# Moving a norm ahead of the last settling, the embeddings' product between the last mixes, and two transposes behind the q/k projections, in an audio tower on one Trainium2 core

## What is computed

```python
def reference(x, ...):
    # tokens: 4096 patches of 200 samples -> spectrum -> two-layer MLP -> 128 features
    fr = jnp.fft.rfft(xp, axis=-1)
    feats = jnp.concatenate([jnp.abs(fr), jnp.angle(fr)], axis=-1)
    h = gelu(feats @ w1 + b1) @ w2 + b2
    # attention: 8 heads of 64, sequences of 256 tokens, 16 of them, sparsemax for softmax
    q, k, v = jnp.split(layernorm(h) @ W_qkv, 3, axis=-1)
    sim = jnp.einsum('bhid,bhjd->bhij', q, k) * SCALE
    z_sorted = jnp.flip(jnp.sort(sim, axis=-1), axis=-1)
    cssv = jnp.cumsum(z_sorted, axis=-1)
    k = jnp.sum(1.0 + r * z_sorted > cssv, axis=-1, keepdims=True)
    tau = (jnp.take_along_axis(cssv, k - 1, axis=-1) - 1.0) / k
    h = h + einsum(jnp.maximum(sim - tau, 0.0), v) @ W_out + b_out
    # experts: 8, each takes its 1024 best tokens of 4096 and adds to them
    return h + experts(layernorm(h))
```

## Time and profile before

| what | us |
|---|---|
| median of 3 runs (918.42 to 922.3) | 920.19 |
| the profiled execution, its time | 916.4 |
| its span, from the first instruction to the last | 914.3 |
| PE busy (share of the span) | 677.6 (74%) |
| DVE busy | 621.5 (68%) |
| ACT busy | 457.8 (50%) |
| POOL busy | 203.4 (22%) |
| POOL's waits for DVE's `more` (line 452), 32 of them | 433.3 |
| ACT's waits for `minus_tau` (line 641), 10 | 67.8 |
| PE's waits for `xn` (line 777), 5 | 26.4 |

### The profile page before, as it was taken

One profiled execution on the slowest core, in us unless ns is written; L12 is line 12 of the kernel. 1 busy time (PEld: TensorE's weight loads), 2 busy tenths in 40 slices (PEclk: granted clock), 3 DMA queues, 4 the chain that ended last, 5 costly groups with the idle time before them and its releaser, 6 DMA issues. The chain is left out here.

```text
span 914.3 us, 13217 instructions
## 1 busy us (share of the span) xinstructions
PE 677.6 (74%) x4060; PEld 451.2 (49%) x4060; DVE 621.5 (68%) x2253; ACT 457.8 (50%) x664; POOL 203.4 (22%) x212
## 2 busy tenths in 40 slices
PE   4788679659969969399999998763331898666680
PEld 2354445355555555166575665542210576555460
DVE  3879886868968967697979879864878665441020
ACT  4868448338756746367778777762000332212210
POOL 1000000001000000001010000001003688888876
PEclk9799789779988988699999998886555799787895
DMA  5200000000000000000000000005000154334433
GB/s 158 80 1 1 1 1 2 1 2 13 2 1 13 1 1 13 1 2 13 1 2 13 1 13 1 13 2 155 1 0 20 41 87 73 48 60 67 70 32 29
DMA packets 34859, 23.73 MB, mean 26 GB/s; under 512 B 8246, under 2 KB 31366, under 8 KB 34768
## 3 DMA queue, kind: packets, MB, share of 16 engines
q0 software_dynamic: 11264, 8.40, 6.8%
q1 hardware_dynamic: 23292, 14.28, 5.7%
q10 hardware_dynamic: 212, 0.08, 0.0%
HBM read 14.36 MB, written 8.39 MB: 25 GB/s over the span
## 5 line engine op out<-in xcount | busy, mean ns | idle before, releaser
L544 ACT ACTIVATE front<-ps 128x1024 f32<-128x1024 f32 x128 | 127.8, 1026 | 38.4 <-PE ps L791 15.0
L641 ACT ACTIVATE front<-front,minus_tau 128x256 f32<-128x256 f32 x256 | 108.7, 497 | 68.9 <-DVE minus_tau L1128 67.8
L544 ACT ACTIVATE back<-ps 128x1024 f32<-128x1024 f32 x72 | 73.8, 1025 | 119.7 <-PE ps L915 105.0
L824 PE MATMUL ps<-ident,front 128*128 128x128 f32 x512 | 78.1, 303 | 50.9 <-ACTq L643 23.6
L452 POOL CROSS_LANE_REDUCE more_all<-more 128x3 int32<-128x3 f32 x32 | 15.2, 474 | 433.3 <-DVEq L1065 433.3
L514 POOL DMA_INDIRECT out_dram<-back x64 | 100.4, 1568 | 24.1 <-issue 23.5
L824 PEld LDWEIGHTS ps<-ident,front 128*128 128x128 f32 x512 | 66.2, 156 | 73.6 <-ACTq L643 39.3
L1046 DVE MATCH_REPLACE8 back<-top,front 128x256 f32<-128x256 f32 x256 | 101.3, 409 | 0.0
L1039 DVE MAX8 top<-front 128x8 f32<-128x256 f32 x256 | 86.8, 411 | 13.9 <-issue 7.7
L1049 DVE MAX8 top<-back 128x8 f32<-128x256 f32 x256 | 86.9, 411 | 2.4
L501 POOL DMA_INDIRECT back<-rows,back x64 | 65.7, 1027 | 74.2 <-issue 70.4
(11 more groups left out here) (170 smaller groups left out, 1027.3 us busy)
## 6 DMA issues: line engine op xcount, KB each, us to landing
back<-in_L_ffn_W_dram SPq DMA_DIRECT2D x16, 256.0 KB
front<-in_x_dram SPq DMA_DIRECT2D x4, 750.0 KB, 4.6
rows<-xn SPq DMA_DIRECT2D x8, 256.0 KB, 2.2
out_dram<-h SPq DMA_DIRECT2D x1, 2048.0 KB, 7.7
back<-rows,back POOLq DMA_INDIRECT x64, 2.6
out_dram<-back POOLq DMA_INDIRECT x64
wqkv<-in_L_attn_W_qkv_dram SPq DMA_DIRECT2D x1, 768.0 KB, 6.2
back<-in_L_ffn_b_dram SPq DMA_DIRECT2D x8, 64.0 KB
```

What stands on the lines that cost most here:

```text
L544: a.activation(dst, ps[s][:, 0:cols], func, **kw).then_inc(sems[f"free{s}"], 1)
L641: a.activation(prob[n % 2][:, r, :], sc[n][:, r, :], ACT.Relu, bias=minus_tau[:, n // 2, n % 2 * 4 + r:n % 2 * 4 + r + 1])
L824: last = nc.tensor.transpose(o[:, a_ * 512 + jb * SEQ + it * P:a_ * 512 + jb * SEQ + (it + 1) * P], prob[n % 2][:, 2 * a_ + it, jb * P:(jb ...
```

## The change

It changes only the two tables. Three things move, and nothing is added or taken away.

- DVE: `embeddings` 0 and `first norm` 0 stand ahead of `settle` 1, which is now the last step of a round. POOL's power for that norm stands behind the reduction for double 1 as before.
- PE and ACT, end of a round: `emb` 1 stands between `mix` 6 and `mix` 7, and ahead of `relu next` 1 on ACT.
- PE and ACT, start of a round: `relu` 2 moves from ahead of `score` 5 to behind `qk` 0, `turn` 2 from behind `col1` to behind `qk` 1, and `relu` 3 from behind `qk` 1 to behind `qk` 2. `turn` 3 stays behind `qk` 3.

```diff
-PLAN = [("score", 4), ("turn", 0), ("out", 1), ("turn", 1), ("relu", 2), ("score", 5), ("mix", 0),
-        ("mix", 1), ("col1", 0), ("turn", 2), ("qk", 0), ("qk", 1), ("relu", 3), ("qk", 2), ("qk", 3),
+PLAN = [("score", 4), ("turn", 0), ("out", 1), ("turn", 1), ("score", 5), ("mix", 0),
+        ("mix", 1), ("col1", 0), ("qk", 0), ("relu", 2), ("qk", 1), ("turn", 2), ("qk", 2), ("relu", 3), ("qk", 3),
...
-        ("hid", 2), ("turn", 6), ("hid", 3), ("turn", 7), ("relu next", 0), ("mix", 6), ("mix", 7),
-        ("relu next", 1), ("emb", 1)]
+        ("hid", 2), ("turn", 6), ("hid", 3), ("turn", 7), ("relu next", 0), ("mix", 6), ("emb", 1),
+        ("mix", 7), ("relu next", 1)]
...
-         ("largest", 1), ("settle", 0), ("thresholds", 1), ("residual", 0), ("settle", 1), ("embeddings", 0),
-         ("first norm", 0)]
+         ("largest", 1), ("settle", 0), ("thresholds", 1), ("residual", 0), ("embeddings", 0), ("first norm", 0),
+         ("settle", 1)]
```

## The result

The changed kernel is slower: 933.05 us median (932.42 to 939.75) against 919.31 (917.55 to 922.3) measured beside it. The ratio is 1.0163, with a 95% interval of 1.0108 to 1.0217. Its profiled execution took 932.73 us, with a span of 930.6; the span before was 914.3.

What follows compares the result with a forecast made beforehand. PE was taken to bound rounds without a refinement, DVE the refined stretches and from mid round 6. Shifts reached +10.6 us after round 5 and +12.6 in round 6; added to 920.2 they gave 932.8 us, range 925 to 941.

Steps and rivals of the forecast that it cites:

- Part 1: Start of a round on PE: idle 0.9 us for `xcur` and 1.26 for each of two relus; +3.4 us per round.
- the sum: Shifts added round by round to +12.6 us at round 6 and the kernel's end, giving 932.8 us.
- Round 0's +3.0: PE's loss at round 0's start, taken below 3.4 us because PE is partly at half clock.
- Part 2: End of a round on PE and ACT: idle 0.37 us, saved 0.24, so +0.1 us.
- Round 3: DVE bounds it through a refinement; PE's 15.04 us of idling absorb the start's loss; shift about +3.6 us.
- The saving ahead of the refinement: DVE, round's end: the settling no longer waits for POOL, so the refinement takes 11.9 us less 1.0.
- A closing without a refinement: DVE, round's end: the gap ahead of `minus_tau` goes; gain some 1.0 us, 1.3 in round 0.
- The tail: Choice of tokens and experts after the rounds: unchanged, so the rounds' shift arrives whole at the kernel's end.
- the rival of the clock: Short PE waits drop TensorE to 1.2 GHz in rounds 1, 4, 5, 6; 937 to 941 us; 20%.
- the second rival: Rounds gain because ACT's chain fits under one `qk` and the start costs nothing; 916 us; 6%.
- The waits for a relu: Sign in rounds 4 and 5: `turn` 2 and `turn` 3 wait 1.2 to 1.4 us each for a relu.
- PE's waits for `xn`: Sign: they shrink from 26.4 us in all to about 7, in rounds 0 and 1.

Runs made afterwards that it cites:

- e5: The changed kernel with `relu` 3 back directly behind `qk` 1's eviction on ACT; ratio 1.0093 to the kernel before.
- e11: The kernel before with only the start of a round changed and the refinement never entered; ratio 0.9571 to the kernel before.
- e3: The kernel before with only `emb` moved between `mix` 6 and `mix` 7, its eviction ahead of `relu next` 1; ratio 0.9990.
- e1: The kernel before with only the start of a round changed (`relu` 2, `turn` 2 and `relu` 3 moved); ratio 1.0150.
- e8: The changed kernel with the refinement never entered; ratio 0.9591 to the kernel before.
- e10: The kernel before with only DVE's order changed and the refinement never entered; ratio 0.9406 to the kernel before.
- e7: The kernel before with the refinement never entered; ratio 0.9353 to the kernel before.
- e6: The changed kernel with `score` 6 ahead of `qk` 0, `score` 7 ahead of `turn` 2, and `relu` 3 behind `turn` 2's eviction; ratio 0.9995 to the kernel before.
- e2: The changed kernel with the start of a round put back as before; ratio 1.0076 to the kernel before.
- e4: The kernel before with only DVE's order changed (`embeddings` and `first norm` ahead of `settle` 1); ratio 1.0150.

## Why the prediction was right, and where it was not

The forecast of 932.8 us met 933.05. It was closer than its steps were.

**Part 1 held.** The chain from a `qk` to its `turn` takes 4.71 us (4.70 in the sum); e5 takes one wait away and gains 1.2 us per round; e11 isolates the part at 3.2 us per round (3.4 in the sum), and rounds 4 and 5 of the changed kernel took 3.4 and 3.5 more than before (3.5 in the sum). Round 0's +3.0 was right too: `largest` 3 waits 6.53 us in place of 3.66, 2.9 more.

```profile
145.12 2.71 DVE L1039 MAX8 top<-front 128x8 f32<-128x256 f32 x8 [6.53 <-ACT front L544]
```

**Part 2 held**: e3 shows nothing, and rounds 4 and 5 of the change are 0.2 longer than e1's.

**The sum, by the eviction of the embeddings** (which the change itself puts 1.0 us earlier; shifts against before, round 1 to 5): forecast +3.7, +2.3, +2.6, +6.1, +9.6; measured +3.0, +2.3, +4.9, +8.3, +11.8 (262.28, 329.79, 417.10, 478.07 and 539.10 against 259.29, 327.52, 412.20, 469.74 and 527.28). Rounds 1, 2, 4 and 5 were sized right to 0.7 us. **Round 3 was the term that failed**: I had it passing its shift on almost unchanged, and it lost another 2.6 us. The rows of round 2's end show why. The saving ahead of the refinement, put at 1.0 us, was 0.6: ahead of its first instruction DVE idles 3.98 us, where it idled 4.60 in the kernel before.

```profile
340.40 0.48 DVE L1072 SCALAR_TENSOR_TENSOR back<-front,tau,zero 128x256 f32<-128x256 f32 x1 [3.98 <-issue]
```

Nearly all of that idle time is not POOL's, as I had taken it. After the change POOL's reduction was over at 329.02, 7 us before the norm's end, and in the kernel before it was already over at 258.92 in round 1, when the residual ended at 259.08 and 4.69 us of idling began. The time goes into the way into the refinement: loads of values, branches and code that stands out of line, which no run takes apart. And the idle time at the loop's turn, 2.57 us in the kernel before, is 3.58 in the change (the line at 351.16 above). That is not the refinement's doing: e8 and e10, never refined, have 3.68 and 3.77 there, and e7 and e11, with the norm last in a round, 2.63. The norm itself took 0.4 more (3.86 from its first instruction to `xn`, where the earlier trace rows have 3.47). Those are 1.8 of the 2.3 us by which round 3's shift was missed. A closing without a refinement saved 0.5 to 0.6 us, not 1.0 to 1.3: from the residual's end to the next residual 6.58 us passed in round 3 and 6.85 in round 0, and after the change 6.10 and 6.27.

**The tail** had been taken as unchanged, and lost 1.6 us: from the last settling of round 6 to the last residual 38.8 us passed before, 40.4 after. The last turn ran at half clock, where in the kernel before it took 1.09 us behind a wait as long (0.71 us), at a granted clock of 1.00 from 612 to 623. From 628 to 634 after the change it was 0.72.

```profile
630.73 1.97 PE L824 MATMUL ps<-ident,front 128*128 128x128 f32 x8 [0.71 <-ACTq L643]
```

So the shift at round 6's end was 15.2 us and in the span 16.3, against 12.6 in the sum: 3.7 us too small. That the median met it is a second thing: I carried over that the profiled execution of before lay 3.8 us under its median, and that of the change lay at its median (0.3 under it). The two errors cancelled, which is luck.

**The rivals.** The clock did not fall in rounds 4 and 5 (1.00 in both windows), so the rival of the clock did not occur there: waits of 0.7, 1.0 and 1.0 us left TensorE at 2.4 GHz. The Trainium skill (TensorE: Matmul & The Clock Gate, section "A second HAM failure mode: psum-queue depth-cycling") has the clock go back and forth where short idle times between groups of matmuls are frequent; rounds 4 and 5 do not show it. The clock did fall behind the longer waits, at 281.78 and 390.19 (1.97 and 1.94 us for a turn), which it did in the kernel before too (1.91 and 1.94 at 276.66 and 384.17), and over the stretches of rounds 1 and 6 it was 0.97 and 0.94 after, 0.96 and 0.94 before. The one new fall found is that of the tail. The gain, the second rival, did not come: e5 and e6 show that the waits must be covered, and with them covered the kernel is level with the one before, not faster. Of the signs named in advance, the rounds of 61 us and DVE's waits for the embeddings (10.6 us in four rounds) came. The waits for a relu show 1.01 us in the rows where 1.2 to 1.4 was named, and are 1.27 by the starts. PE's waits for `xn` in the rounds vanished but for 5.03 and 1.75 us in rounds 0 and 1, but they sum to 11.6 and not to about 7: the 26.4 of before held a wait of 4.82 behind the rounds, which the sign had left out and which is still there.

**What I had not seen** is that DVE's new order alone would cost as much as the start of the round. The prediction had its parts (it said that DVE waits before it settles, and what is queued behind that) but priced them only beside the late `relu` 2, where they cost little more than e1. That the two parts share their loss was found by e1, e2 and e4, not by the sum.

## What to carry to other kernels

When a transpose is moved behind a product, ask what that product's eviction delays on the other engine: a turn that waits for a relu needs as much work of PE's between the product and itself as the way over the other engine takes (here 3.0 us from the product's end: 2.6 for eviction and relu, the rest for handing over; one more product covers 1.7), and work that needs neither (here two score products) fills the gap. A repair that moves work must be read by stage as well: here a part of its gain came from another round than the one repaired. An engine that must wait for another's result should first do the long work that doesn't need it: to take the sum that waits for the embeddings ahead of a settling puts a refinement of 11 us in series with the wait. And where two parts of a change are measured alone, their costs need not add: here 13.8 and 13.8 us gave 15.

## What was new about the hardware

Where a settling branched into its refinement, DVE idled 3.98 and 4.21 us ahead of the first instruction (rounds 2 and 1 after the change), although POOL's reduction was long over. In round 0, where DVE's work is written out and not in a loop, this idle time was 2.64 us. What of it is the load of the value, the branches or the code out of line is not shown.

DVE's idle time at the loop's turn was 2.57 us with the norm as a round's last step and 3.58 with the settling last. Without refinements it was the same (2.63 in e7, 3.68 in e8). Why is not shown.

PE's rows show a wait behind a 128x512 product about 0.25 us too short (1.01 us, where the starts leave 1.27): distances between starts are what to compare.

And the same instruction ahead of round 0 ended up to 6 us apart between profiled executions (122.30 to 128.94), more than several of the effects measured here.
